# Register loads of a runtime loop on two engines: all at the turn's start, or in small parts spread over the turn

## What is computed

```python
def reference(x, src, dst, edge_type_32, ...):
    edge_index = jnp.stack([src, dst])
    x = _layernorm(x + _L0_gnn_ref(x, edge_index, ...), axis=-1)
    x = _layernorm(x + _L1_gnn_ref(x, ..., edge_index, edge_type_32), axis=-1)
    x = _layernorm(x + _L2_gnn_ref(x, edge_index, ...), axis=-1)
    x = _layernorm(x + _L3_gnn_ref(x, edge_index, ...), axis=-1)
```

## Time and profile before

| | |
|---|---|
| time, median of 3 runs | 5093.97 us (5093.39 to 5096.05) |
| span of the profiled execution, first to last instruction | 4502.2 us |
| what lies around the span, if the profiled execution took the median | 591.8 us |
| stretch of the counting loop | 93.8 us to about 933 us of the span |
| turns | 49 of 12 steps, and 2 steps behind them |

### The profile page before, as it was taken

How to read it: one execution, slowest core, us unless ns; L and a number is a source line. 1 busy time by engine, 2 the same in 40 slices (tenths; PEclk the granted TensorE clock), 3 DMA queues, 4 the chain that set the end, 5 groups by cost and what they waited for, 6 DMA issues and landing times. The chain is left out here.

```text
span 4502.2 us, 61902 instructions
## 1 busy us (share of the span) xinstructions
PE 3040.5 (68%) x16266; PEld 2267.0 (50%) x16267; DVE 3392.0 (75%) x7111; ACT 2104.7 (47%) x5569; POOL 1731.0 (38%) x1694
## 2 busy tenths in 40 slices
PE   5888888887255555555435555555546888779878
PEld 2444444466255555555435555555535888435434
DVE  8888888842588888888668888888858885444345
ACT  4555555551344444444345555555527885132231
POOL 0000000062577777777277777777700000021010
PEclk7999999988555555555555555555555555889988
DMA  0000000030322222222122222222230000000000
GB/s 21 0 0 0 0 0 0 0 161 1 69 67 67 67 67 67 67 67 69 31 71 66 69 67 67 67 67 67 63 162 1 1 1 2 11 4 1 4 9 8
DMA packets 136540, 183.42 MB, mean 41 GB/s; under 512 B 48763, under 2 KB 110116, under 8 KB 135396
## 3 DMA queue, kind: packets, MB, share of 16 engines
q0 software_dynamic: 50048, 77.77, 7.6%
q1 hardware_dynamic: 85348, 84.60, 6.9%
q10 hardware_dynamic: 896, 18.10, 0.9%
HBM read 158.02 MB, written 22.33 MB: 40 GB/s over the span
## 5 line engine op out<-in xcount | busy, mean ns | idle before, releaser
L1121 POOL DMA_INDIRECT adjacency<-dram_table,sorted_dst x1564 | 1555.9, 995 | 672.7 <-issue 425.8
L1148 PE MATMUL banks<-adjacency 128*128 x3520 | 779.5, 419 | 463.6 <-ACT adjacency L1180 463.6
L1148 PEld LDWEIGHTS banks<-adjacency 128*128 128x128 f32 x3520 | 759.3, 332 | 507.2 <-issue 507.2
L1193 ACT ACTIVATE adjacency<-adjacency 128x128 f32<-128x128 bf16 x1760 | 537.9, 397 | 50.2 <-DVE adjacency L1241 50.0
L1286 DVE TENSOR_REDUCE adjacency<-adjacency 128x512 f32<-128x2048 f32 x110 | 399.5, 3632 | 125.7 <-ACT adjacency L1193 125.7
L1180 ACT ACTIVATE adjacency<-adjacency 128x2048 f32<-128x2048 f32 x110 | 210.3, 1912 | 565.2 <-DVE adjacency L1218 565.2
L1921 PE MATMUL banks<-adjacency,cheb_parts 128*128 128x512 f16 (+1 forms) x2100 | 437.0, 367 | 52.5 <-ACTq L97 31.7
L665 ACT ACTIVATE adjacency<-banks 128x400 f32 x590 | 296.9, 503 | 318.6 <-PE banks L637 313.5
L1173 PE MATMUL banks<-ident,adjacency 128*128 128x128 f32 x440 | 122.6, 434 | 447.5 <-DVE adjacency L1286 447.5
L2190 POOL TENSOR_TENSOR cheb_y<-cheb_y,cheb_gain 128x512 f32<-128x512 f32 (+1 forms) x21 | 24.1, 1150 | 984.2 <-DVE cheb_y L2106 984.2
L634 PE MATMUL banks<-cell_hot,src_hot 128*128 128x400 f16 x1180 | 319.7, 353 | 74.0 <-DVE cell_hot L572 73.0
(11 more groups left out here) (497 smaller groups left out, 6100.8 us busy)
## 6 DMA issues: line engine op xcount, KB each, us to landing
adjacency<-dram_src_rows SPq DMA_DIRECT2D x440, 128.0 KB
adjacency<-dram_table,sorted_dst POOLq DMA_INDIRECT x1564, 2.5
dram_adjacency<-adjacency ACTq DMA_DIRECT2D x1, 17600.0 KB, 46.3
adjacency<-dram_adjacency SPq DMA_DIRECT2D x1, 15387.5 KB, 39.4
dram_table<-adjacency SPq DMA_DIRECT2D x8, 291.0 KB, 6.1
adjacency<-dram_adjacency SPq DMA_DIRECT2D x1, 2212.5 KB, 14.5
dram_nodes<-x_nodes SPq DMA_DIRECT2D x1, 800.0 KB, 4.3
x_nodes<-dram_nodes SPq DMA_DIRECT2D x1, 800.0 KB, 5.8
```

Source lines behind the costliest of these rows:

```text
L1121: pool.indirect_dma_start(ring[:, j % (RG * TG), :], None, dram["table"], bass.IndirectOffsetOnAxis(ap=S.dst_i[:, j:j + 1], axis=0)).then_ ...
L1148: ins = pe.matmul(sums[b % 2][:, s * W1:(s + 1) * W1], reach[:, b % 3, s, t, :], ring[:, bass.ds(at_r[s], TG), :][:, t, 0:W1], start=(t == ...
L1193: ins = act.activation(reach[:, b % 3, s, t, :], hot[:, b % 2, s, :, t], ACT.Identity, scale=-FAR, bias=score[:, b % 2, s * TG + t:s * TG ...
```

## The change

VectorE no longer loads 12 values at the start of a turn, but 3 there and 3 more ahead of steps 3, 6 and 9. ScalarE's three loads of 12 values become six of 6 values: the values of `at_j` are loaded ahead of steps 0 and 6, and those of `next_g` and `next_j` inside steps 0 and 6, just before the first `act_cell` that uses them. TensorE's loop isn't touched.

```diff
-    RING, TURN, EACH, AHEAD_R, CELLS = 3, 12, 3, 4, 6
+    RING, TURN, EACH, AHEAD_R, CELLS, HELP = 3, 12, 3, 4, 6, 6
...
     def dve_turn(dve, turn, n):
         first = turn * TURN
-        at_g = load_row(k, dve, table[0:1, 0, bass.ds(first, n)], 0, TP - TGA)
+        some = min(n, EACH)
+        at_g = load_row(k, dve, table[0:1, 0, bass.ds(first, some)], 0, TP - TGA)
         for i in range(n):
             r = i % RING
+            if i and i % EACH == 0:
+                at_g = at_g + load_row(k, dve, table[0:1, 0, bass.ds(first + i, some)], 0, TP - TGA)
             dve.wait_ge(hot_read.sem, i + 1)
...
     def act_turn(act, turn, n):
         first = turn * TURN
-        at_j = load_row(k, act, table[0:1, 1, bass.ds(first, n)], 0, NWIN - 1)
-        next_g = load_row(k, act, table[0:1, 0, bass.ds(first + AHEAD_R, n)], 0, TP - TGA)
-        next_j = load_row(k, act, table[0:1, 1, bass.ds(first + AHEAD_R, n)], 0, NWIN - 1)
+        at_j, next_g, next_j = (), (), ()
         for i in range(n):
+            some = min(HELP, n - i)
+            if i % HELP == 0:
+                at_j = at_j + load_row(k, act, table[0:1, 1, bass.ds(first + i, some)], 0, NWIN - 1)
             act.wait_ge(done.sem, i + 1)
             act.activation(A4[:, :, bass.ds(at_j[i], 1), :], psum[i % RING][:, 0:NB * WIN].rearrange("b (a o w) -> b a o w", w=WIN, o=1),
                            ACT.Copy).then_inc(copied.sem, 1)
             if n >= EACH and i % EACH == 0:
                 act_part(act, i // EACH)
+            if i % HELP == 0:
+                next_g = next_g + load_row(k, act, table[0:1, 0, bass.ds(first + AHEAD_R + i, some)], 0, TP - TGA)
+                next_j = next_j + load_row(k, act, table[0:1, 1, bass.ds(first + AHEAD_R + i, some)], 0, NWIN - 1)
             act_cell(act, next_g[i], next_j[i], (i + AHEAD_R) % CELLS)
```

## The result

The changed kernel takes 5264.55 us (median of 4 runs, 5261.09 to 5266.41), the kernel before 5093.68 us in the same comparison. The ratio is 1.0334, 95% interval 1.032 to 1.0348: 171 us slower. The prediction had the direction, 5188 us and a range up to 5260 us, so the time lies outside it by 5 us, and the loss is 1.8 times the forecast one.

A forecast was written before the change was run, and what follows sets the result against it. The ring of TensorE's L637 and ScalarE's L665 bounds the counting loop: 16.47 - 0.51 + 2 x 1.36 + 0.30 (clock) = 18.98 us a turn, 1.91 more than 17.07; 49 turns add 94 us, giving 5188 us, range 5108 to 5260.

The forecast's parts named there:

- The ring of L637 and L665: Counting loop: TensorE's L637 and ScalarE's L665 wait for each other step after step, giving 16.47 us a turn without the clock.
- VectorE's part: VectorE's four loads of 3 values, 0.79 us each, cost nothing, being hidden by work it has queued.
- ScalarE's turn start: One load ahead of the first wait instead of three lets L665 come in time: 0.51 us a turn gained.
- inside the steps: ScalarE's loads of next_g and next_j in steps 0 and 6 delay the ring by 1.36 us twice a turn.
- The pair at step 0: The loads of next_g and next_j between L653 and L656, each of 0.70 us, delay the ring by 1.36 us.
- the price of six values at step 6: A ScalarE load of six values was three accesses, taken as 0.70 us, bounds 0.308 and 0.782 us.
- the formula: Delay by ScalarE's pair of loads inside a step: 2T - 0.04 for loads of length T.
- Nothing for `at_j`: ScalarE's load ahead of step 6 costs nothing, hidden in 0.71 us mean idle time beside L656's 0.29 us.
- The clock term: Time a turn loses to stretches at 0.50 of the clock: 0.30 us kept of the kernel before's 0.60 us.
- My rival of the clock: The clock falls oftener in the loop, two low stretches a turn: 5259 to 5275 us; chance 0.15.
- The floor under a small load: The skill's floor of about 600 ns per `tensor_load`, set aside for the rows; by it some 5170 us.
- What lies around the span: 591.8 us of the kernel before's 5093.97 us lie outside the profile's 4502.2 us span, untouched by the change.

The follow-up runs named there:

- e3: Kernel before, ScalarE's loads of next_g and next_j, still of 12 values, moved behind the part copy of step 0: 5119.95 us against 5094.92, ratio 1.0048.
- e4: The changed kernel, but ScalarE reads 8 values at a time from a multiple of 4 and leaves the surplus: 5143.55 us against 5094.92 before.
- e6: As e5, with TensorE also loading 4 values at the turn's start and in steps 3 and 6: 4428.32 us against 4502.87 before.
- e1: VectorE's part of the change alone, ScalarE's loads as in the kernel before: 5094.99 us against 5094.92, ratio 0.9999.
- e2: ScalarE's part of the change alone, VectorE's load as in the kernel before: 5263.75 us, ratio 1.0331 to the kernel before.
- e10: The changed kernel with HELP 4 instead of 6, so ScalarE's loads are fours on a boundary: 5076.79 us against 5091.44 before.
- e5: Kernel before, ScalarE loading aligned fours: three at the turn's start, others ending steps 1, 2, 4 and 5: 4469.85 us against 4502.87.
- e8: As e4, with the pair of loads moved ahead of ScalarE's wait for the L609 matmuls: 4500.44 us against 4502.87 before, ratio 0.9994.

## Why the prediction was right and where it failed

**The ring of L637 and L665 bounds the loop: right.** A turn was put together as 16.47 us; e3 and e4 came to 17.57 and 18.09 us for sums without the clock of 17.48 and 18.08, and e6 to 15.44 for 15.45.

**VectorE's part costs nothing: right** (e1), with loads of 0.745 us for a forecast of 0.79.

**At ScalarE's turn start 0.51 us are gained, inside the steps more is lost: right** in kind and place, as the rows above show. The pair at step 0 measured 2.53 - 1.10 = 1.43 us for the forecast 1.36, since six values took 0.756 us and not 0.70.

**The failed step is the price of six values at step 6.** I read a load as 4 + 1 + 1 accesses wherever it starts, and set 0.782 us, what 12 values take, as the upper bound. But 12t + 6 and 12t + 10 are no multiples of 4. These loads are six accesses, 1.331 us. The pair cost 3.42 - 1.10 = 2.32 us in place of 1.36, and the load of `at_j` ahead of step 6, which I had at nothing, 1.69 - 1.43 = 0.26 us. The two together, 2.58 us, are near the formula's 2 x 1.33 - 0.04 = 2.62: L669 came late, and L656 behind it then found its matmuls done. Together the two steps cost 1.43 + 2.32 + 0.26 = 4.01 us and not 2.72: 1.29 us a turn, 63 us over 49 turns.

Nothing for `at_j` also rested on a misread wait. The 0.71 us were a mean into which the long waits at the turns' starts had gone; ahead of a group's first L665 the kernel before waits only 0.42 us:

```profile
514.21 0.50 ACT L665 ACTIVATE adjacency<-banks 128x400 f32 x1 [0.42 <-PE banks L637]
```

With L656's 0.29 us there is room for 0.71 us, and even the load as forecast wanted 0.82.

**The clock term was too small too.** 16.47 - 0.51 + 4.01 = 19.97 us leave 20.51 - 19.97 = 0.54 us a turn for it, about what it was before (0.60) and not the 0.30 that I kept: 12 us. 5188 + 63 + 12 = 5263 us stand against the measured 5264.55 us. My rival of the clock had 5259 to 5275 us, but isn't what happened, and that the measured time lies in it is chance: the granted clock is 0.94 in the loop after and 0.93 before, and a low stretch still comes in two turns of three, at 0.71 us each about 0.5 us a turn. When a low stretch comes stays open. In the change it always followed the longest pause; in e2, with the same loads on ScalarE, 32 of 34 begin behind the pause at the turn's start. With pauses added it nearly vanished in e3 and e4 (0.99). What is shown is only that it was gone when the pause at the turn's border was 0.5 us shorter (e6).

**The floor under a small load.** The Trainium skill, "DMA: Bandwidth & Descriptors", section "Latency and other measured facts", gives about 600 ns for a `tensor_load`. The traces do not agree: the 444 loads of e10, nearly all of 4 values, have a median of 0.308 us. An estimate from that floor is 9 x 0.6 = 5.4 us for e10's nine loads a turn; they take 9 x 0.308 = 2.8. The three of before take 3 x 0.782 = 2.3 us, and e10 is 15 us faster than before.

**What lies around the span** was wrong, as told above, without touching the sum.

## What to carry to other kernels

Ask of a load that moves not only how long it is but what its sequencer stands behind: ahead of a wait that lasts anyhow it is hidden for as long as the wait lasts (e5, e8), behind that wait it is paid in full if the next instruction is on the ring (the change, e4). Before costing a split, look at where the pieces start, not only at how many values they hold; the cheap piece here was four values on a multiple of four. A row for one size is no upper bound for another one with a different start.

## What the runs showed that I had not expected

- Time of a load of register values, ScalarE: 4 on a multiple of 4 places 0.308 us, 8 there 0.546, 6 there 0.756, 12 there 0.782, but 6 that start two places further 1.331 us. VectorE: 3 in 0.745, 12 in 0.846, 11 that start one place behind a multiple of 4 in 2.514 us.
- The same kernel took 4502.87, 5091.44 and 5094.92 us on three chips. All but a few of the 592 us between the profiles of the two kinds are in the attention stage, 2174 to 2762 us with busy times within 4%. The runs don't show why.
